# A graph transformer layer pair on one core: register loads for ten edge blocks at once, setup by groups of tiles, first units split by ACT and DVE, last expert by groups of tokens

## The reference, cut to what matters

```python
xn = _layernorm(x, axis=-1)
x = x + _L0_gnn_ref(xn, edge_index, ...) + _L0_mix_ref(xn[None], ...)[0]
x = x + _L0_ffn_ref(_layernorm(x, axis=-1)[None], ...)[0]
xn = _layernorm(x, axis=-1)
x = x + _L1_gnn_ref(xn, edge_weight, edge_index_t, ...) + _L1_mix_ref(xn[None], ...)[0]
x = x + _L1_ffn_ref(_layernorm(x, axis=-1)[None], ...)[0]
```

```python
gate = softmax(x @ Wg); top 2 of 8, scaled to sum 1
y = sum over e of weight[e] * (gelu(x @ W1[e] + b1[e]) @ W2[e] + b2[e])
```

## Time and profile before

| | us |
|---|---|
| median of 3 runs | 1845.51 |
| lowest, highest | 1834.01, 1851.74 |
| profiled execution | 1841.88 |
| its span | 1840.2 |
| mean granted clock of TensorE | 0.949 of full speed |

### The profile page before, as it was taken

One profiled execution on the slowest core, in us unless ns is written; L12 is line 12 of the kernel. 1 busy time (PEld: TensorE's weight loads), 2 busy tenths in 40 slices (PEclk: granted clock), 3 DMA queues, 4 the chain that ended last, 5 costly groups with the idle time before them and its releaser, 6 DMA issues.

```text
span 1840.2 us, 23095 instructions
## 1 busy us (share of the span) xinstructions
PE 1604.1 (87%) x8839; PEld 1225.3 (67%) x8839; DVE 1001.3 (54%) x1749; ACT 420.1 (23%) x798; POOL 328.4 (18%) x198
## 2 busy tenths in 40 slices
PE   1798877786989799979987999977999998599998
PEld 0677767666757677867765788866767656365665
DVE  6777677777963762384264666773245314641222
ACT  2422111222311220120113332333225001311121
POOL 2101012052210111012010122120211100003554
PEclk9899999997989899989997999988999999789999
DMA  3213223441230010001020010110101230555332
GB/s 109 96 37 108 84 96 118 138 131 36 81 129 0 24 40 24 1 23 42 11 80 24 23 46 24 47 46 1 46 24 71 89 117 20 204 187 164 48 66 36
DMA packets 51266, 123.72 MB, mean 67 GB/s; under 512 B 8003, under 2 KB 28378, under 8 KB 44151
## 3 DMA queue, kind: packets, MB, share of 16 engines
q1 hardware_dynamic: 14735, 66.64, 10.2%
q10 hardware_dynamic: 26570, 45.35, 7.0%
q0 software_dynamic: 9856, 10.28, 3.3%
HBM read 92.71 MB, written 40.22 MB: 72 GB/s over the span
## 4 chain that ended last, share of the span: by engine, by line
PE 73%; DVE 13%; DMA 7%; issue 3%; ACT 2%; DVEq 1%; PEld 0%; SPq 0%; POOL 0%; PEldq 0%; POOLq 0%; ACTq 0%
PE ps L598 8%; PE ps L599 8%; PE ps L600 8%; DMA arena<-d_kv 4%; PE ps L656 4%; PE ps L2143 4%; PE ps L658 4%; PE ps L609 4%; PE ps L2846 4%; PE ps L610 3%; PE ps L611 3%; PE ps L898 3%; PE ps L2820 3%; PE ps L787 2%; DMA arena<-d_w 1%
## 5 line engine op out<-in xcount | busy, mean ns | idle before, releaser
L2702 POOL CAST wslot<-arena 128x2048 fp32r<-128x2048 f32 x29 | 57.8, 1995 | 1093.7 <-PEq L2788 1072.0
L598 PE MATMUL ps<-wslot,XH 128*125 128x512 f32 (+2 forms) x560 | 216.1, 386 | 8.6 <-DVE XL L1364 7.0
L599 PE MATMUL ps<-wslot,XH 128*125 128x512 f32 (+2 forms) x560 | 213.4, 381 | 0.0
L600 PE MATMUL ps<-wslot,XL 128*125 128x512 f32 (+2 forms) x560 | 213.0, 380 | 0.0
L609 PE MATMUL ps<-XH,wslot 128*128 128x500 f32 (+1 forms) x336 | 124.0, 369 | 33.7 <-DVE XL L1364 31.9
L2704 POOL TENSOR_TENSOR wslot<-arena,wslot 128x2048 fp32r<-128x2048 f32 x29 | 135.0, 4655 | 2.3
L2143 PE MATMUL ps<-arena 125*128 x1330 | 96.5, 228 | 40.5 <-DVE arena L2398 31.5
L598 PEld LDWEIGHTS ps<-wslot,XH 128*125 128x125 f32 x560 | 105.4, 188 | 35.8 <-DVE XL L1364 8.7
L656 PE MATMUL ps<-CTr,Hhi 125*128 125x500 f32 (+1 forms) x360 | 125.0, 361 | 0.0
L610 PE MATMUL ps<-XH,wslot 128*128 128x500 f32 (+1 forms) x336 | 123.0, 366 | 0.0
L611 PE MATMUL ps<-XL,wslot 128*128 128x500 f32 (+1 forms) x336 | 121.8, 363 | 0.0
(11 more groups left out here) (427 smaller groups left out, 3096.2 us busy)
## 6 DMA issues: line engine op xcount, KB each, us to landing
arena<-in_units SPq DMA_DIRECT2D x29, 1024.0 KB, 4.8
arena<-in_units SPq DMA_DIRECT2D x8, 2048.0 KB, 12.2
d_w<-arena ACTq DMA_DIRECT2D x10, 625.0 KB
d_wt<-arena ACTq DMA_DIRECT2D x10, 625.0 KB, 4.0
rows<-in_rows ACTq DMA_DIRECT2D x22, 256.0 KB, 3.9
d_kv<-V SPq DMA_DIRECT2D x20, 250.0 KB
arena<-d_kv SPq DMA_DIRECT2D x20, 250.0 KB
arena<-d_wt ACTq DMA_DIRECT2D x2, 2441.4 KB
```

Of the source, the lines that this page charges most:

```text
L598: pe.matmul(o, lhsT=xh[:, k, s], rhs=H4[:, k, 0:nw], start=k == 0, stop=False, skip_group_check=True)
L599: pe.matmul(o, lhsT=xh[:, k, s], rhs=L4[:, k, 0:nw], start=False, stop=False, skip_group_check=True)
L600: last = pe.matmul(o, lhsT=xl[:, k, s], rhs=H4[:, k, 0:nw], start=False, stop=k == K - 1, skip_group_check=True)
```

## The change

Parts, in the order in which the program meets them:

1. **Loads by order.** All of x comes on SP's queue by groups: tiles 0 to 3 (1.0 MB), then unit 0, then tiles 4 to 7 and 8 to 9. ACT's queue has the edge weights, wg and cols. The two edge lists share one semaphore.
2. **Setup by groups.** Statistics, root, scale, normalisation and the store of x are done for each group of tiles. The equality over all edge columns (pre[:, :, 0]) comes after the statistics of the first group and unit 0, right before the loop over three rounds: turned tiles of a group, statistics of the next, one weighting in two halves with a query output between. DENSE has three q jobs, not two, after the first turned tiles, and then three and six. The one-hots of block 0 are written before the last five query outputs.
3. **Units 0 to 3** are copied by ACT (split_high) and subtracted by DVE (unit_low): 0 in the setup, 1 before the loop and at block 1, 2 at blocks 11 and 12, 3 at blocks 22 and 24. POOL keeps the later units; the additions to ktot and of bo come before them in its list.
4. **Register loads.** Ten blocks (twenty registers) at once, before the loop and behind the visits of blocks 9, 19 and 29.
5. **Group sums** of DVE come one block later, behind the one-hots; the last group's behind the attended rows.
6. **Keys and values.** Two semaphores, so that two pairs are under way; K^T V in blocks 27 to 36, key sums in block 38, base loaded at block 38.
7. **Expert 0:** four u jobs, the six wb jobs, two u jobs, then d. The gate's top values ahead of the b2 addition.
8. **Last expert:** u 0 to 3, d of group 0, u 4 and 5, d of group 1, turned tiles t6 of group 0, d of group 2.

```diff
-DENSE = ([("turn", t) for t in range(4)] + [("q", i) for i in range(2)] + [("turn", t) for t in range(4, 8)]
-         + [("q", i) for i in range(2, 5)] + [("turn", t) for t in range(8, NT)] + [("q", i) for i in range(5, 12)]
+DENSE = ([("turn", t) for t in range(4)] + [("q", i) for i in range(3)] + [("turn", t) for t in range(4, 8)]
+         + [("q", i) for i in range(3, 6)] + [("turn", t) for t in range(8, NT)] + [("q", i) for i in range(6, 12)]
...
-IN_LOOP.update({25 + t: ("kv", t) for t in range(NT)})
-IN_LOOP[36] = ("ks", 0)
+IN_LOOP.update({27 + t: ("kv", t) for t in range(NT)})
+IN_LOOP[38] = ("ks", 0)
...
-       + all_of("u0", 6) + all_of("wb", 6) + all_of("d0", NT)
+       + all_of("u0", 4) + all_of("wb", 6) + [("u0", 4), ("u0", 5)] + all_of("d0", NT)
...
+       + all_of(LAST_U, 4) + [(LAST_D, t) for t in GROUPS[0]] + [(LAST_U, 4), (LAST_U, 5)] + [(LAST_D, t) for t in GROUPS[1]]
+       + turned("t6")[0] + [(LAST_D, t) for t in GROUPS[2]] + by_group("q", 4)[0]
...
         def load_bounds(eng, regs, g):
-            eng.reg_load(regs, bnd_i[0:1, 8 * g:8 * g + 8])
+            eng.reg_load(regs, bnd_i[0:1, 2 * PER * g:2 * PER * g + 2 * PER])
...
+            def unit_low(u):
+                dve.wait_ge(unit_high, u + 1)
+                dve.tensor_tensor(wL[unit_slot(u)], wraw, wH[unit_slot(u)].bitcast(F32), ALU.subtract).then_inc(w_ready, 1)
...
+            x_stats(0)
+            dve.wait_ge(turn_full, 2)
+            dve.tensor_reduce(bnd_c[0:2 * NB, 0:1], ps[0:2 * NB, 2, 0:NCH], X_AXIS, ALU.max).then_inc(bounds_ready, 1)
+            x_spread(0)
...
+            x_scale(0)
+            bounds_to_registers()
+            unit_low(0)
             own(dve.tensor_tensor(pre[:, 0:NCH, 0, :], iota_d[0:TP, :].unsqueeze(1).to_broadcast([TP, NCH, BW]),
                                   dlow.unsqueeze(2).to_broadcast([TP, NCH, BW]), ALU.is_equal))
...
+            for i in range(3):
+                if i < 2:
+                    if i == 0:
+                        dve.wait_ge(bounds_ready, 4)
+                        bounds = load_bounds(dve, regs, 0)
+                        for t in GROUPS[0]:
+                            turn_low(t)
+                    x_stats(i + 1)
+                    x_spread(i + 1)
+                    if i == 0:
+                        dve.wait_ge(exp_done, 2)
+                    next_part(i)
+                    x_scale(i + 1)
+                else:
+                    next_part(i)
+                weigh(i, 0)
+                q_out(3 * i)
+                weigh(i, 1)
                 settle()
+                if i < 2:
+                    q_out(3 * i + 1)
+                    q_out(3 * i + 2)
+                    for t in GROUPS[i + 1]:
+                        turn_low(t)
+            dve.sem_inc(pre_ready, 1)
...
+            for i in range(VIS):
+                one_hot(oh[i], bounds[0][0] + i, 0).then_inc(oh_ready, 1)
+            for i in range(7, 12):
+                q_out(i)
...
+                if b % PER == PER - 1 and b + 1 < NB:
+                    bounds = load_bounds(dve, regs, (b + 1) // PER)
+                if b in (1, 12, 24):
+                    unit_low({1: 1, 12: 2, 24: 3}[b])
...
+                if b >= 5 and b % 4 == 1:
+                    dve.wait_ge(w_reduced, b - 1)
+                    group_sums((b - 5) // 4)
...
+            def split_high(u):
+                act.wait_ge(w_loaded, 16 * (u + 1))
+                if u:
+                    act.wait_ge(w_used, u)
+                act.activation(wH[unit_slot(u)], wraw, ACT.Copy).then_inc(unit_high, 1)
+
+            def norm_group(g):
+                t0, t1 = GROUPS[g][0], GROUPS[g][-1] + 1
+                act.wait_ge(x_var, g + 1)
+                act.activation(std[0:TP, t0:t1], var[:, t0:t1], ACT.Sqrt, bias=lneps[0:TP, :]).then_inc(x_std, 1)
+                if g == 0:
+                    split_high(0)
+                act.wait_ge(x_scaled, g + 1)
+                for t in GROUPS[g]:
+                    norm_x(t)
+                act.wait_ge(x_normed, t1)
+                act.dma_start(d_xn[:, t0:t1, :], R1t[:, t0:t1, :]).then_inc(xn_stored, 16)
...
+                if (kind, i) in (("q", 0), ("q", 3)):
+                    norm_group(1 + i // 3)
...
-                        if t:
-                            sp.wait_ge(kv_loaded, 32 * t)
-                        sp.dma_start(K0t[:, t, :], d_kv[:, 0, t, :]).then_inc(kv_loaded, 16)
-                        sp.dma_start(R2t[:, t, :], d_kv[:, 1, t, :]).then_inc(kv_loaded, 16)
+                        if t >= 2:
+                            sp.wait_ge(kv_loaded[t % 2], 32 * (t // 2))
+                        sp.dma_start(K0t[:, t, :], d_kv[:, 0, t, :]).then_inc(kv_loaded[t % 2], 16)
+                        sp.dma_start(R2t[:, t, :], d_kv[:, 1, t, :]).then_inc(kv_loaded[t % 2], 16)
...
                 sp.dma_start(wraw, A["units"][u]).then_inc(w_loaded, 16)
+                if u == 0:
+                    load_x(1)
+                    load_x(2)
```

DVE's side of the last expert:

```diff
+                up(0)
+                for i in range(1, 4):
+                    up(i)
+                    gelu_low(i - 1)
+                if e == E0 - 1:
+                    gelu_low(3)
+                    down(GROUPS[0])
+                    spreads(0)
+                    up(4)
+                else:
+                    up(4)
+                    gelu_low(3)
+                up(5)
+                gelu_low(4)
                 gelu_low(5)
...
+                    scales(5, 0)
+                    down(GROUPS[1])
+                    spreads(1)
+                    low_cols(5, "t6", GROUPS[0])
+                    down(GROUPS[2])
+                    scales(5, 1)
+                    spreads(2)
+                    scales(5, 2)
+                    low_cols(5, "t6", GROUPS[1])
+                    low_cols(5, "t6", GROUPS[2])
```

More of the change, by code:

```diff
@@ L431, in program @@
         rows_loaded = sem("rows_loaded")
-        x_in = [sem(f"x_in{i}") for i in range(2)]
+        x_in = [sem(f"x_in{i}") for i in range(3)]
         x_var = sem("x_var")
@@ L446, in program @@
         staged_out = [sem(f"staged_out{i}") for i in range(2)]
-        kv_loaded = sem("kv_loaded")
+        kv_loaded = [sem(f"kv_loaded{i}") for i in range(2)]
         ktot_added = sem("ktot_added")
@@ L750, in stream_pe, with weight_job, up_jobs, down_jobs @@
                       skip_group_check=True).then_inc(mx_full, 1)
+            def weight_job(i):
+                c0, cw = CH[i // 2]
+                o = begin(("wb", i))
+                for t in range(c0 // TP, (c0 + cw) // TP):
+                    k = NT * (i % 2) + t
+                    last = pe.matmul(o[:, TP * t - c0:TP * t - c0 + TP],
+                                     lhsT=wtop[0:TP, k:k + 1].to_broadcast([TP, 128]),
+                                     rhs=ident[0:TP, 0:TP], start=True, stop=True, skip_group_check=True)
+                last.then_inc(mx_full, 1)
+            def up_jobs(e, w, some):
+                Hw, Lw = first_half(w)
+                for i in some:
+                    cols_job((f"u{e}", i), i // 2, i % 2, Hw, Lw)
+            def down_jobs(e, w, some):
+                Hw, Lw = second_half(w)
+                for t in some:
+                    pe.wait_ge(hidden_low, 6 + 6 * e + 2 * (1 + min(t // 4, 2)))
+                    rows_job((f"d{e}", t), HH, HL, t, Hw, Lw, 2)
             for e in range(E0):
                 w = unit()
-                Hw, Lw = first_half(w)
-                for i in range(6):
-                    cols_job((f"u{e}", i), i // 2, i % 2, Hw, Lw)
+                up_jobs(e, w, range(4))
                 if e == 0:
@@ L758, in stream_pe @@
                     for i in range(6):
-                        c0, cw = CH[i // 2]
-                        o = begin(("wb", i))
-                        for t in range(c0 // TP, (c0 + cw) // TP):
-                            k = NT * (i % 2) + t
-                            last = pe.matmul(o[:, TP * t - c0:TP * t - c0 + TP],
-                                             lhsT=wtop[0:TP, k:k + 1].to_broadcast([TP, 128]),
-                                             rhs=ident[0:TP, 0:TP], start=True, stop=True, skip_group_check=True)
-                        last.then_inc(mx_full, 1)
-                Hw, Lw = second_half(w)
-                for t in range(NT):
-                    pe.wait_ge(hidden_low, 6 + 6 * e + 2 * (1 + min(t // 4, 2)))
-                    rows_job((f"d{e}", t), HH, HL, t, Hw, Lw, 2)
+                        weight_job(i)
+                if e == E0 - 1:
+                    down_jobs(e, w, GROUPS[0])
+                up_jobs(e, w, range(4, 6))
+                if e < E0 - 1:
+                    down_jobs(e, w, range(NT))
+                else:
+                    down_jobs(e, w, GROUPS[1])
+                    turn_group("t6", 5, 0, lambda t: R1t[:, t, :])
+                    down_jobs(e, w, GROUPS[2])
                 unit_done()
@@ L1653, in gelu_low, with up @@
```

(7 more changed lines are left out.)

285 lines of the change are left out of this document (130 added, 155 removed).

## The result

| | us |
|---|---|
| changed kernel, median of 20 runs | 1826.12 (1822.71 to 1839.38) |
| kernel before, measured beside it, median of 20 | 1841.95 |
| ratio, 95% interval | 0.9924 (0.9906 to 0.9941), so 14 us less |
| profiled execution of the changed kernel, its span | 1839.34, 1837.6 |

The forecast was 1812, a gain of 33.3. The measured time lies in the range, but the gain is less than half of what was forecast. The profiled execution is one of the slowest of its kernel, 13 us above the median; where that comes from stands further down, and until then its trace is read stage by stage, not by its end.

What follows compares the result with a forecast made beforehand. PE bounds the kernel (73% of the chain), so only shortening its pauses helps. Gains 11 + 8 + 2.8 + 3.5 + 8 = 33.3 us take the profiled 1841.88 to 1808.6; the median, 3.6 higher, is 1812, range 1796 to 1830.

Steps and rivals of the forecast that it cites:

- Setup: Ahead of the loop: x in ordered groups starts queries near 33 us and ends the first block at 81.6, gaining 11 us.
- Edge loop: From first to last block end: reload pauses and old register loads go, new DVE and POOL work comes, net gain 8 us.
- I take 2.5, nearest to the latency: Edge loop: length taken for one twenty-value register load, between 1.97 us (latency alone) and 4.9 (per value).
- 1 + 1 + 2.5 = 4.5: Edge loop: total cost in us of the three twenty-value loads in blocks 9, 19 and 29, behind the one-hots.
- 13.6: Edge loop: us gained by two key and value pairs under way and their earlier start, removing two PE pauses and slow clock.
- POOL's ten additions: Edge loop: key-sum additions said to fall newly into a loop that DVE paces, costing 2 us.
- Behind the loop: After the last block: the last group's sums leave the path to the attended rows, gaining 2.8 us.
- First expert: Weight rows after four jobs, not six, pauses partly filled, gate's top values moved ahead of an addition: gain 3.5 us.
- Last expert: Reordered down jobs bring the second layer's first query job to 1239.3 us instead of 1247.48, gaining 8 us.
- Rival 1: Early starts are handed back: setup keeps 5, loop keeps 3, gain 19 us, time 1827; chance 0.22.
- Rival 3: DVE becomes the loop's bound; its bursts pause PE and lower its clock, costing 37 us, time 1849; chance 0.03.
- the ten places: Edge loop: blocks 1, 9, 12, 13, 19, 24, 25, 29, 33 and 37, where DVE has a burst of 2.2 to 5.4 us.

Runs made afterwards that it cites:

- experiment 2: Changed kernel with its twenty-value register loads moved to be the last step of blocks 9, 19 and 29 on both engines: 1824.4 us, ratio 0.9912.
- 5: Changed kernel with the two limits of one block loaded at the head of each block, instead of ten blocks at once: 1809.4 us, ratio 0.9811.
- Experiment 3: Kernel before with one edit, limits of ten blocks loaded at once at the changed kernel's places, the first still ahead of the loop: 1849.8 us, ratio 1.0051.
- experiment 12: Changed kernel with one-block loads, plus a group's two sums split over two blocks and unit 2's subtraction later: 1805.0 us, ratio 0.9798.
- 10: Changed kernel with one-block loads, plus the last group's sums put back ahead of the attended rows: 1809.8 us, ratio 0.9815.
- the second trace: Trace of the changed kernel run once more with nothing changed: 1829.5 us, ratio 0.9930 to the kernel before.
- experiment 9: Changed kernel with one-block loads, plus the last expert back in the order of the kernel before: 1822.1 us, ratio 0.9879.
- experiment 4: Changed kernel with limits loaded for two blocks at once, four values as every second block's first step: 1810.4 us, ratio 0.9829.
- four at once: Changed kernel with limits loaded for four blocks at once, as each fourth block's first step: 1826.7 us, and 1825.6 when run again.

## Why the prediction was right or wrong

- **Setup, 11 (5 to 16): right.** 13.3 us. Queries at 31.1 (33 forecast), first block end at 79.6 (81.6). The first tiles of x landed 2.4 us later than I had it, the rest was quicker.
- **Edge loop, 8 (0 to 16): wrong in sign**, 9.6 us longer by the trace. The step that failed is "I take 2.5, nearest to the latency", and "1 + 1 + 2.5 = 4.5" for the three loads of twenty values. The least was 4.5 us, near the 4.9 "per value" that I had as the upper end, and DVE's at block 9 took 10.0. Not only the size was off: the sum had DVE's load alone and no term for PE's, which stands between the last visit and the drain; and none for the slow clock behind it, though the sum charged 2.5 a time for it elsewhere. Ten at once against one at once is 272.2 against 255.3: 16.9 us in place of 4.5, of which 2.5 are the place (experiment 2) and 14.4 the length (2 against 5). Experiment 3 shows it without the rest of the change.
- That 255.3 lies beside the 254.6 forecast is luck in part: two pairs gave 7.5 of the 13.6 (8; the delay's part is open), while short loads replaced both the 4.5 and the loads of eight, and experiment 12 shows 8.5 us more in bursts of DVE that the forecast had let stand.
- The 2 us for "POOL's ten additions" rest on a wrong reading. They were not new: in the trace before they already ran in the loop, from 259.4 to 330.7 us. The DVE operations beside them took 3.1 us longer in sum than their like did there, and 4.3 in the changed kernel, so 1.1 more.
- The Trainium skill (Runtime: NRT & Kernel Launch, Instruction fetch mechanics) gives a TENSOR_LOAD some 200 ns for each register, "even for bulk", for loads that the runtime makes from HBM. The 0.22 us for each value here, loaded by the kernel from its own tile, agree. An estimate from that figure of the Trainium skill, 20 times 0.2, would have been 4.0 us, and I did not weigh it.
- **Behind the loop, 2.8 (1 to 3): wrong**, nothing (10). I took the sums off DVE's path without asking what the attended rows waited for; it was ACT's issuing of DMAs, 2.90 us here and 2.11 before. The sums then stood in the open behind them. The lead even shrank, from 3.7 us at the last block end to 2.1 at 400 us and 1.2 at 945; what took it stays open.
- **First expert, 3.5 (1 to 5): right.** The lead grew from 1.2 to 5.4 us over the gate and it, 4.1; in the second trace 6.2, above the range.
- **Last expert, 8 (4 to 10): the mechanism right, the size for one place only.** The first query job of the second layer came at 1233.72, 13.8 us sooner, of which 5.4 was there already: 8.4. But PE then waits 6.46 us for the low columns of the second group (the expectation of 9 calls it the third), and the end of the query jobs keeps 4.5 (5.6 in the second trace, 6.5 by experiment 9). PE's timeline, as in the earlier trace rows:

```profile
1225.77 3.59 PE L595 MATMUL ps<-ident,arena 125*128 125x125 f32 x16 [5.36 <-ACT arena L1081]
...
1233.72 0.47 PE L613 MATMUL ps<-XH,wslot 128*128 128x500 f32 x1 [0.82 <-DVE XL L1386]
...
1252.98 0.76 PE L613 MATMUL ps<-XH,wslot 128*128 128x500 f32 x1 [6.46 <-DVE XL L1386]
```

- **Rivals.** Rival 1's time (1827) is the measured one, but not by its mechanism: setup kept its start. Rival 3, with its 0.03, had more of the mechanism than the forecast: the changed loop has six pauses of PE over 2.7 us, each with the lower level behind it. Three stand behind the loads (6.14, 4.98 and 5.55 us), three behind DVE's other work: at block 13, where DVE waited 3.71 us for ACT's copy of unit 2, at block 25 behind the subtraction of unit 3, and at block 38 behind the output of K^T V and a group's sums. The kernel before had five of 2.69 to 4.68 us in its loop, two of them for keys and values, and the total stayed below rival 3's price. PE's timeline of the changed kernel:

```profile
168.27 1.99 PE L2179 MATMUL ps<-arena 125*128 x17 [5.30 <-DVE arena L2442]
...
258.38 1.88 PE L2179 MATMUL ps<-arena 125*128 x16 [3.10 <-DVE arena L2442]
...
341.87 2.31 PE L2179 MATMUL ps<-arena 125*128 x20 [3.40 <-DVE arena L2442]
```

  Of the forecast's signs of being wrong, "loads of 5 us" came true, and so did the pauses of over 2.7 us, one at each of six of the ten places.

## What to carry to other kernels

Price a register load by its values, not by its instruction: here it held back all that stood behind it on its engine for that time (8.52 us in the chain through block 9), and where two engines hand each other buffers within a block, as these do, one long stop on either was paid in full, plus the clock that PE lost by it. Split such work until a piece fits into the time that an engine has to spare in one step: 40 loads of 0.5 us beat 4 of 5 us at the same place in the block by 14.4 us of the loop and 15 of the time (experiments 5 and 2). When work is moved off a path, first find what the waiting engine really waits for; and give a first job's gain only as far as the next wait lets it through.

## What the runs showed of the hardware

- A register load does not have a fixed length. Four values took 0.96 us at the least and up to 4.68 (DVE, experiment 4), twenty 4.49 to 10.05. The long ones stood mostly where a store to memory was under way: one of the weights, 640 KB (at 127.6 us in the changed kernel, at 105 and 162 us in experiment 4), or a smaller one alone. In the kernel before three loads of eight values took 3.43 us on DVE, where 1.84 is the least, each 0.1 us behind SP's issue of a 250 KB store of keys or values (191.7, 220.6 and 247.4 us), with nothing else moving. The DMA view of the first (191.8 to 195.2 us; packets, MB, share):

```profile
q1 hardware_dynamic: 128, 0.26, 24.6%
...
d_kv<-V SPq DMA_DIRECT2D x1, 250.0 KB
```

  Not every store did it: at 279.0 us in experiment 4 one of 640 KB was under way beside the reload of keys and values, and four values took 0.98 us. That the stores cause it was not tried.
- PE can run at its lower level while it is busy without a break: 39 of 40 us busy at a mean clock of 0.70 (four at once, first trace), and the stage cost 11 us more than in another execution of the same program. In the changed kernel's trace it lay from 1620 to 1650 us, where PE is busy all 30 us at a mean clock of 0.61; ahead of it PE was busy for 20 of 40 us (1540 to 1580) and then 35 of 40. The 40 us had a mean clock below 0.9 in nine of the 16 traces, and its length changed from one execution to the next. A difference below some 10 us between two kernels of this program should not be read off one trace's end.
